# GpSimd takes token differences and two squared keys, and the value stage is put in a new order, in a two-layer kernel on one Trainium2 core

## The chip, the core and the metric

The kernel runs on one core of one Trainium2 chip. The metric is device time in microseconds (us) of one execution. A core has TensorE (PE, matmuls, with PEld for its weight loads), VectorE (DVE), ScalarE (ACT), GpSimd (POOL) and the queues that start transfers (SP). The engines run side by side and wait for each other on semaphores. Each takes its own instructions in the order in which the program lists them, so what stands behind a waiting instruction waits too.

## What is computed

The input is 2048 tokens of 128 channels, kept with channels on the partitions. Four stages follow each other, each with a residual and a layer norm. The change touches the second and its surroundings:

```python
x = _layernorm(x + _L0_attn_ref(x, ...))      # heads attend among themselves; ends in one 128x128 matrix
x = _layernorm(x + _L0_ffn_ref(x, W_r, W_k, W_v, mu_r, mu_k))
x = _layernorm(x + _L1_attn_ref(x, ...))      # two small MLPs, then a scan-like sum over 16 states
x = _layernorm(x + _L1_ffn_ref(x, ...))       # gated MLP with 512 hidden channels, two gelu layers

# _L0_ffn_ref
x_prev = concatenate([zeros, x[:, :-1]])
xr = mu_r * x + (1 - mu_r) * x_prev
xk = mu_k * x + (1 - mu_k) * x_prev
out = sigmoid(xr @ W_r) * (square(relu(xk @ W_k)) @ W_v)
```

## The kernel before, in words

The tokens are cut into four chunks of 512 (`c` = 0 to 3), and every stage works chunk by chunk. There is no planner: the order on each engine is written out by hand as a list of calls, and each call is one or two instructions on one 128x512 tile, with a wait ahead and a semaphore increment behind.

- **First norm (y1).** TensorE makes y1 of a chunk (L212 to L214), ScalarE squares it (`square`, L528), TensorE averages it over the channels (L1235), ScalarE makes 1/sqrt of that by Ln and Exp (`rstd_of`, L533 and L535).
- **Token shift.** For each chunk VectorE does `first_input` (x1 = PSUM times rstd, L887), `token_step` (x1 minus x1 of the token before, L892, both operands in SBUF) and two mixes (L897: step times mu plus x1 of the token before, both tensors in SBUF): the key mix K(c) and the receptance mix R(c). `mixed` counts the mixes.
- **Value stage.** TensorE: `key(c)` (L1255) on K(c), `receptance(c)` (L1259) on R(c), `value(c)` (L1265) on the squared key. ScalarE: `key_relu` (L552), `key_square` (L557), Tanh of the receptance (L547). VectorE: `gate` (L926, L929). Then TensorE centres (`y2`, L1235) and averages the squares (`y2_variance`, L1235), ScalarE does Ln and Exp (L533, L535), VectorE makes x2 and splits it in a high and a low part (`second_input`, L935, L876, L878), on which `layer1(c)` of the third stage starts (L212 to L214).
- **Weights of the last stage.** `wf_raw` holds 11 blocks of 128x512. GpSimd rounds each to its high part (`tensor_copy`, L378 for blocks 0 to 3, L383 for 4 to 10) as soon as the transfer has landed, and VectorE subtracts (`fill_low(f)`, L833, two SBUF operands). ScalarE takes the magnitude of the low parts in four calls (`low_magnitude`, L522). `state_weights` (L851 on VectorE) makes 128x96 matrices for the scan out of a small one. These are put in the gaps of the VectorE and ScalarE lists.
- **Scan.** From about 74 us on GpSimd, VectorE, ScalarE and TensorE share a sum over the states.

Of the kernel before, what the change touches and what calls it, by code (L numbers as in the profile page):

```python
# [23 lines left out]
ALU = mybir.AluOpType  # L24
# [4 lines left out]
CH = 512  # L29
HEADS = 16  # L30
HD = P // HEADS
NS = 16
# [4 lines left out]
LN_EXP = "natural_log_exp_and_others"  # L37
# [7 lines left out]
def build(nc, t, out):  # L45
# [4 lines left out]
    NCH = T // CH  # L50
# [8 lines left out]
    with ctx:  # L59
# [3 lines left out]
        def sem(name):  # L63
            return ctx.enter_context(nc.semaphore(name))
# [39 lines left out]
        nfill = 3 + 2 * KH  # L104
# [13 lines left out]
        def sb_and_f32(name, width):  # L118
# [7 lines left out]
        x1r, x1_f32 = sb_and_f32("x1r", T + 2)  # L126
        xr = sb("xr", [P, 2, T], F32R)
        bx1, bs1, bs2, bs3, bx2, bxt, bdl = [sb(n, [P, T]) for n in ("bx1", "bs1", "bs2", "bs3", "bx2", "bxt", "bdl")]
# [13 lines left out]
                for b in (bx1[:, :], bx2[:, :], bs2[:, :], x1_f32[:, 0, 2:], x1_f32[:, 1, 2:],  # L142
# [31 lines left out]
        sc_mm, sm_ok, smax_ok, exp_ok, srec_ok, prob_ok, u_mm, u_ok, m_mm, mix_ok = [  # L174
            sem(n) for n in ("sc_mm", "sm_ok", "smax_ok", "exp_ok", "srec_ok", "prob_ok", "u_mm", "u_ok", "m_mm",
                             "mix_ok")]
        y1_mm, y1_sq, y1_var, y1_ln, y1_rs, x1_ok, step_ok, mixed = [
            sem(n) for n in ("y1_mm", "y1_sq", "y1_var", "y1_ln", "y1_rs", "x1_ok", "step_ok", "mixed")]
        key_mm, rec_mm, th_ok, relu_ok, k2_ok, v_mm, p_ok, y2_ok, y2_mm, y2_sq, y2_var, y2_ln, y2_rs = [
            sem(n) for n in ("key_mm", "rec_mm", "th_ok", "relu_ok", "k2_ok", "v_mm", "p_ok", "y2_ok", "y2_mm", "y2_sq",  # L180
                             "y2_var", "y2_ln", "y2_rs")]
# [21 lines left out]
        def cs(c):  # L203
            return slice(c * CH, (c + 1) * CH)
# [139 lines left out]
        def _(pool):  # L344
            g = nc.gpsimd
# [31 lines left out]
            for f in range(f0, f1):  # L377
                g.tensor_copy(wf[:, f, 0, :], wf_raw[:, f, :]).then_inc(fill_hi0, 1)  # L378
            pool.wait_ge(fill_hi0, FILL)
            for f in range(FILL, nfill):  # L380
                if f % FILL == 0:
                    pool.wait_ge(ld_f[f // FILL], 16)
                g.tensor_copy(wf[:, f, 0, :], wf_raw[:, f, :]).then_inc(fill_hi, 1)  # L383
            pool.wait_ge(fill_hi, nfill - FILL)

            def c_parts(c):

# [63 lines left out]
            for i in range(NCH // 2):  # L451
                for stage in range(3):
                    for k in range(2):
                        for o in range(KH):
                            n = mtile(i, stage, k, o)
# [9 lines left out]
        def _(act):  # L465
# [50 lines left out]
            def low_magnitude(j):  # L516

                f0, f1 = LOW_SPANS[j]
                act.wait_ge(fill_lo, f1)
                if j:  # L520
                    act.wait_ge(low_ok, j)
                a.activation(magnitudes[:, 0:(f1 - f0) * HID].rearrange("p (f c) -> p f c", c=HID),  # L522
                             full(wf[:, f0:f1, 1, :]), ACT.Abs, accum_out=low_max[:, j:j + 1]).then_inc(low_ok, 1)

            def square(mm_sem, sq_sem, c):

                act.wait_ge(mm_sem, c + 1)
                a.activation(bs1[:, cs(c)], ps[:, 4 + c, :], ACT.Square).then_inc(sq_sem, 1)  # L528
# [14 lines left out]
            def receptance(c):  # L543

                act.wait_ge(rec_mm, c + 1)
                act.wait_ge(y1_var, c + 1)
                a.activation(bs1[:, cs(c)], ps[:, c, :], ACT.Tanh, scale=0.5).then_inc(th_ok, 1)  # L547

            def key_relu(c):

                act.wait_ge(key_mm, c + 1)
                a.activation(bs2[:, cs(c)], ps[:, 4 + c, :], ACT.Relu).then_inc(relu_ok, 1)  # L552

            def key_square(c):

                act.wait_ge(relu_ok, c + 1)
                a.activation(bs3[:, cs(c)], bs2[:, cs(c)], ACT.Square).then_inc(k2_ok, 1)  # L557
# [26 lines left out]
                a.activation(bs1[:, s], bs1[:, s], ACT.Ln, bias=1.0).then_inc(d_ln, count)  # L584

            act.preload_act_table(ACT.Tanh)
            receptance(0)
            key_relu(0)
            key_relu(1)
            key_square(0)  # L590
            receptance(1)
            key_square(1)
            low_magnitude(0)
            receptance(2)
            key_relu(2)
            key_relu(3)
            key_square(2)
            key_square(3)
            receptance(3)
            square(y2_mm, y2_sq, 0)  # L600
            square(y2_mm, y2_sq, 1)
            act.preload_act_table_set(LN_EXP)
            rstd_of(y2_var, y2_ln, y2_rs, 0)
            square(y2_mm, y2_sq, 2)
            rstd_of(y2_var, y2_ln, y2_rs, 1)
# [139 lines left out]
        def _(dve):  # L745
            v = nc.vector
# [80 lines left out]
            def fill_low(f):  # L827

                if f < FILL:
                    dve.wait_ge(fill_hi0, f + 1)  # L830
                else:
                    dve.wait_ge(fill_hi, f - FILL + 1)
                v.tensor_tensor(wf[:, f, 1, :], wf_raw[:, f, :], full(wf[:, f, 0, :]),  # L833
                                ALU.subtract).then_inc(fill_lo, 1)

            dve.wait_ge(sc_mm, 1)
            dve.wait_ge(mask_ok, 2)
            v.scalar_tensor_tensor(sm[:, :], ps[:, 0, 0:P], float(1.0 / np.sqrt(T)), mask[:, :], ALU.mult,
# [8 lines left out]
            def state_weights(n0, n1):  # L847

                dve.wait_ge(h0f_ok, 3)
                for n in range(n0, n1):  # L850
                    v.tensor_scalar(h0sel[:, n, :], h0T[:, :], one_state[:, n:n + 1], None, ALU.mult).then_inc(h0sel_dve, 1)  # L851

            fill_low(0)
            state_weights(9, 11)

            dve.wait_ge(m_mm, 1)
            dve.wait_ge(consts, 6)
# [8 lines left out]
            v.tensor_tensor(w1[:, :, 1, :], w1raw[:, 0:3:2, :], full(w1[:, :, 0, :]), ALU.subtract).then_inc(w1_lo, 1)  # L866
            v.tensor_scalar(amin[:, :], amat[:, :], 0.0, None, ALU.min).then_inc(a_ok, 1)
            v.tensor_scalar(amax[:, :], amat[:, :], 0.0, None, ALU.max).then_inc(a_ok, 1)
            for f in range(1, 5):
                fill_low(f)  # L870

            def split(full_sem, hi_sem, lo_sem, full_buf, dst, c):
# [8 lines left out]
            def shifted(i, c, shift):  # L881
                return x1_f32[:, i, c * CH + shift:(c + 1) * CH + shift]

            def first_input(c):

                dve.wait_ge(y1_rs, c + 1)
                v.tensor_tensor(shifted(0, c, 2), ps[:, 4 + c, :], bs2[:, cs(c)], ALU.mult).then_inc(x1_ok, 1)  # L887

            def token_step(c):

                dve.wait_ge(x1_ok, c + 1)
                v.tensor_tensor(bx2[:, cs(c)], shifted(0, c, 2), shifted(0, c, 1), ALU.subtract).then_inc(step_ok, 1)  # L892

            def token_mix(c, mu, dst):

                dve.wait_ge(step_ok, c + 1)
                v.scalar_tensor_tensor(dst, bx2[:, cs(c)], vec[:, mu:mu + 1], shifted(0, c, 1), ALU.mult,  # L897
                                       ALU.add).then_inc(mixed, 1)

            def mixes(c):  # L900
                token_mix(c, MU_K, bx1[:, cs(c)])
                token_mix(c, MU_R, shifted(1, c, 2))

            first_input(0)
            token_step(0)
            mixes(0)
            first_input(1)
            first_input(2)
            token_step(1)
            mixes(1)  # L910
            first_input(3)
            token_step(2)
            mixes(2)
            token_step(3)
            mixes(3)

            def transformed(c):

# [13 lines left out]
            def second_input(c):  # L932

                dve.wait_ge(y2_rs, c + 1)
                v.tensor_tensor(bx2[:, cs(c)], ps[:, 4 + c, :], bs2[:, cs(c)], ALU.mult).then_inc(x2_ok, 1)  # L935
                split(x2_ok, x2_hi, x2_lo, bx2, lambda c: parts(xr, c), c)

            gate(0)
            gate(1)
            state_weights(11, 12)  # L940
            gate(2)
            gate(3)
            state_weights(12, 14)
            second_input(0)
            second_input(1)
            fill_low(5)
            second_input(2)
            fill_low(6)
            fill_low(7)
            second_input(3)  # L950

            def bounded(c):

# [57 lines left out]

            transformed(0)
            transformed(1)
            fill_low(8)
            bounded(0)
            fill_low(9)
            bounded(1)
            state_weights(14, NS)
            step_size(0)
            c_times_b(0)  # L1020
            step_size(1)
            fill_low(10)
            c_times_b(1)
            dve.wait_ge(a_ok, 2)
            dve.wait_ge(d_ps, 2)
# [158 lines left out]
        def _(pe):  # L1184
# [68 lines left out]
            def key(c):  # L1253
                pe.wait_ge(mixed, 2 * c + 1)
                m.matmul(ps[:, 4 + c, :], w0raw[:, 1, :], bx1[:, cs(c)], start=True, stop=True).then_inc(key_mm, 1)  # L1255

            def receptance(c):
                pe.wait_ge(mixed, 2 * c + 2)
                m.matmul(ps[:, c, :], w0raw[:, 0, :], x1_f32[:, 1, c * CH + 2:(c + 1) * CH + 2], start=True,  # L1259
                         stop=True).then_inc(rec_mm, 1)  # L1260

            def value(c):
                pe.wait_ge(k2_ok, c + 1)
                pe.wait_ge(th_ok, c + 1)
                m.matmul(ps[:, c, :], w0raw[:, 2, :], bs3[:, cs(c)], start=True, stop=True).then_inc(v_mm, 1)  # L1265

            def y2(c):
                over_channels(y2_ok, y2_mm, centre, bs3, 4, c)

            def y2_variance(c):  # L1270
                over_channels(y2_sq, y2_var, ones, bs1, 0, c)
# [92 lines left out]
            key(1)  # L1364
            receptance(1)
            key(2)
            value(0)
            receptance(2)
            value(1)
            key(3)  # L1370
            receptance(3)
            y2(0)
            y2(1)
            value(2)
            value(3)
            y2_variance(0)
            y2_variance(1)
            y2(2)
            y2(3)
            y2_variance(2)  # L1380
            pe.wait_ge(w1_lo, 1)
# [244 lines left out]
```

## Time and profile before

| | us |
|---|---|
| median of the three runs | 255.01 |
| lowest and highest | 253.63 and 256.02 |
| the profiled execution | 255.75 |
| its span, first to last instruction | 254.0 |
| mean granted clock of TensorE, as a share of 2.4 GHz | 0.950 |

The profile has for each engine its busy time and share of the span, the chain of work that ended last (followed back from the last instruction to whatever released it), and a timeline of instructions with their start, duration, and the idle time before them with the engine that ended it. An instruction's duration runs from its start on the engine to its end and takes in any time in which it is held up inside the engine.

### The profile page before, as it was taken

The numbers are of one execution on the slowest core, as the hardware profiler recorded it, in microseconds if no ns is written. First come the engines' busy times: TensorE is split into PE (matmuls) and PEld (weight loads), VectorE is DVE, ScalarE is ACT, GpSimd is POOL, SyncE is SP. The second block draws the span as 40 slices with busy tenths as digits, with TensorE's granted clock in tenths as the row PEclk, the third lists the DMA queues.
The fourth block names the chain that finished last, engine by engine and source line by source line (L and its number), as shares of the span: only waits on it lengthen the run. The fifth ranks groups of instructions, "written<-read, shape, count | busy, mean of one in ns | idle before, by whom it ended". The sixth has DMA issues, their size and how long they took to land.

```text
span 254.0 us, 2617 instructions
## 1 busy us (share of the span) xinstructions
PE 228.5 (90%) x839; PEld 146.9 (58%) x839; DVE 206.9 (81%) x330; ACT 180.5 (71%) x247; POOL 127.1 (50%) x103
## 2 busy tenths in 40 slices
PE   7898888999999659997868999999999899999981
PEld 7898533445542225543434646578888678888860
DVE  3996889596699899969989989980699997996454
ACT  4766499799897999979989956369843743643433
POOL 3362000000079987999999953473344478055220
PEclk9999999999999957999795999999999999999996
DMA  6960000000000000000000000000000000110002
GB/s 135 389 253 1 1 0 0 3 0 0 0 0 0 3 4 0 0 0 0 3 1 1 0 0 0 0 3 0 0 0 3 0 0 0 45 41 0 0 1 83
DMA packets 4847, 6.16 MB, mean 24 GB/s; under 512 B 384, under 2 KB 2656, under 8 KB 4832
## 3 DMA queue, kind: packets, MB, share of 16 engines
q1 hardware_dynamic: 4832, 5.97, 7.1%
q8 instruction: 8, 0.13, 0.2%
q14 instruction: 7, 0.06, 0.1%
HBM read 4.92 MB, written 1.05 MB: 24 GB/s over the span
## 4 chain that ended last, share of the span: by engine, by line
PE 44%; DVE 26%; ACT 9%; POOL 9%; issue 8%; DMA 2%; SPq 0%; ACTq 0%; POOLq 0%; DVEq 0%
PE ps L1454 8%; PE ps L1455 8%; PE ps L1340 7%; PE ps L1316 3%; POOL bs L420 3%; DVE tr L1088 3%; PE ps L1235 2%; DMA bx<-in_x_dram 2%; POOL bxt L399 2%; PE ps L212 2%; DVE xr L1085 2%; DVE tr L1085 2%; PE ps L213 1%; PE ps L214 1%; PE ps L1281 1%
## 5 line engine op out<-in xcount | busy, mean ns | idle before, releaser
L731 ACT ACTIVATE bs<-ps,vec 128x512 f32<-128x512 f32 x48 | 31.7, 691 | 37.2 <-PE ps L1455 36.0
L1316 PE MATMUL ps<-tr,h0sel 96*128 96x512 f32 x64 | 26.5, 527 | 11.0 <-issue 3.0
L389 POOL CAST tr<-bs 96x512 fp32r<-96x512 f32 x4 | 2.8, 695 | 51.1 <-ACT bs L628 50.9
L1316 PEld LDWEIGHTS ps<-tr,h0sel 96*128 96x128 f32 x64 | 12.4, 212 | 24.1 <-issue 12.2
L1454 PE MATMUL ps<-xr,wf 128*128 128x512 f32 x64 | 25.4, 396 | 0.0
L1455 PE MATMUL ps<-xr,wf 128*128 128x512 f32 x64 | 25.3, 396 | 0.0
L460 POOL TENSOR_TENSOR xr<-bs,xr 128x512 fp32r<-128x512 f32 x12 | 16.1, 1349 | 14.0 <-DVE xr L1085 14.0
L460 POOL TENSOR_TENSOR tr<-bs,tr 128x512 fp32r<-128x512 f32 x8 | 10.9, 1360 | 22.3 <-DVE tr L1085 22.3
L1085 DVE CAST tr<-bs 128x512 fp32r<-128x512 f32 x16 | 7.4, 487 | 13.3 <-ACT bs L731 13.2
L460 POOL TENSOR_TENSOR x1r<-bs,x1r 128x512 fp32r<-128x512 f32 x12 | 13.5, 1129 | 9.3 <-DVE x1r L1085 9.3
L445 POOL TENSOR_TENSOR bs<-bs 128x1024 f32<-128x1024 f32 x6 | 14.3, 2384 | 3.7 <-DVE bs L995 3.6
L1454 PE MATMUL ps<-tr,wf 128*128 128x512 f32 x40 | 15.7, 394 | 0.2 <-DVE tr L1088 0.2
L1340 PE MATMUL ps<-bx,centre 128*128 128x512 f32 x28 | 16.0, 706 | 0.0
L1455 PE MATMUL ps<-x1r,wf 128*128 128x512 f32 x40 | 15.7, 393 | 0.0
L1455 PE MATMUL ps<-tr,wf 128*128 128x512 f32 x40 | 15.7, 392 | 0.0
L1454 PE MATMUL ps<-x1r,wf 128*128 128x512 f32 x40 | 15.7, 391 | 0.0
L1454 PE MATMUL ps<-lr,wf 128*128 128x512 f32 x32 | 14.5, 453 | 1.0 <-DVE bs L1070 1.0
L1190 PE MATMUL ps<-ones 128*128 128x128 f32 x86 | 13.0, 314 | 1.1 <-DVE ones L747 1.1
L1455 PEld LDWEIGHTS ps<-xr,wf 128*128 128x128 f32 x64 | 12.0, 188 | 2.9
L1454 PEld LDWEIGHTS ps<-xr,wf 128*128 128x128 f32 x64 | 12.0, 188 | 2.8
L981 DVE SCALAR_TENSOR_TENSOR bx<-ps,amax,bx 128x1024 f32<-128x1024 f32 x11 | 13.6, 1275 | 0.0
L641 ACT ACTIVATE bx<-bdl,amin 128x1024 f32<-128x1024 f32 x12 | 13.0, 1138 | 0.2 <-PE ps L1340 0.2
(221 smaller groups left out, 667.8 us busy)
## 6 DMA issues: line engine op xcount, KB each, us to landing
wf_raw<-in_w_mlp_dram SPq DMA_DIRECT2D x2, 1024.0 KB, 9.2
bx<-in_x_dram SPq DMA_DIRECT2D x4, 256.0 KB, 5.7
out_dram<-bdl SPq DMA_DIRECT2D x4, 256.0 KB, 2.3
wf_raw<-in_w_mlp_dram SPq DMA_DIRECT2D x1, 768.0 KB, 11.8
bdl<-in_w_ssm_dram SPq DMA_DIRECT2D x1, 448.0 KB, 8.5
wa<-in_w_attn_dram SPq DMA_DIRECT2D x1, 256.0 KB, 2.7
w0raw<-in_w_ffn_dram SPq DMA_DIRECT2D x1, 192.0 KB, 7.9
h0T<-in_state_dram SPq DMA_DIRECT2D x1, 48.0 KB, 5.8
```

Source lines behind the costliest of these rows:

```text
L420: g.tensor_tensor(vbuf[e % NB][:, j, :], vbuf[e % NB][:, j, :], zmax, ALU.add).then_inc(e_vp, 1)
L445: g.tensor_tensor(b[:, 0, :], b[:, 0, :], b[:, 1, :], ALU.add).then_inc(e_add, 1)
L460: g.tensor_tensor(sl[:, 1, o, :], hbuf[k][:, o, :], full(sl[:, 0, o, :]), ALU.subtract).then_inc(m_lo_p, 1)
L641: a.activation(vbuf[e % NB][:, j, :], bdl[:, pair_tokens(e)], ACT.Exp, scale=amin[:, n:n + 1]).then_inc(e_t, 1)
L731: a.activation(hbuf[k][:, o, :], ring(mbank(i, stage, k, o)), ACT.Gelu if stage else ACT.Silu, scale=vec[:, s + o:s + o + 1]).then_inc(m_a ...
L981: v.scalar_tensor_tensor(tile, delta_ps, amax[:, n:n + 1], tile, ALU.mult, ALU.add).then_inc(e_v, 1)
L1085: v.tensor_copy(sl[:, 0, o, :], hbuf[k][:, o, :]).then_inc(m_hi, 1)
L1190: last = m.matmul(ps[:, bank, P:2 * P], ones[:, :], ones[:, :], start=True, stop=True)
L1316: last = m.matmul(ps[:, 2 * j + k, :], h0sel[:, group_states(e)[j], :], tr[0:96, 0, cs(2 * (e // NG) + k)], start=True, stop=True)
L1340: last = m.matmul(ps[:, SUM_BANK + k, :], centre[:, :], vbuf[e % NB][:, j, k * CH:(k + 1) * CH], start=(e % NG == 0 and j == 0), stop=(e % ...
L1454: m.matmul(dst, wf[:, f, 0, wo], x[0], start=start, stop=False)
L1455: last = m.matmul(dst, wf[:, f, 0, wo], x[1], start=False, stop=stop and not low_weights)
```

## The change

1. `token_step` of chunks 1 to 3 leaves VectorE. GpSimd makes them (`bx2`), each after `x1_ok` of its chunk, and the mixes of these chunks wait on GpSimd's semaphore `step_pool`. Chunk 0 stays on VectorE.
2. The squared keys of chunks 1 and 3 leave ScalarE. GpSimd multiplies the tile by itself after the relu (`k2_pool`).
3. GpSimd waits for the mixing matrix (`mix_ok` 3) between block 3 and block 4 of its weight copies.
4. VectorE's list has `fill_low` 0 and 1 ahead of the scores, 2 and 3 behind the softmax, 4 to 7 (with five `state_weights`) ahead of `first_input(0)`, and 8 to 10 behind `second_input(3)`; the last one is no longer between the two `c_times_b` ahead of the scan.
5. ScalarE's first `low_magnitude` is ahead of the first norm, and its value stage begins with the keys.
6. VectorE's mixes and TensorE's value stage are in a new order.

```diff
@@ gpsimd
             pool.wait_ge(fill_hi0, FILL)
+            pool.wait_ge(mix_ok, 3)
             for f in range(FILL, nfill):
                 ...
                 g.tensor_copy(wf[:, f, 0, :], wf_raw[:, f, :]).then_inc(fill_hi, 1)
             pool.wait_ge(fill_hi, nfill - FILL)
+            for c in range(1, NCH):
+                pool.wait_ge(x1_ok, c + 1)
+                g.tensor_tensor(bx2[:, cs(c)], x1_f32[:, 0, c * CH + 2:(c + 1) * CH + 2],
+                                x1_f32[:, 0, c * CH + 1:(c + 1) * CH + 1], ALU.subtract).then_inc(step_pool, 1)
+            for c in range(1, NCH, 2):
+                pool.wait_ge(relu_ok, c + 1)
+                g.tensor_tensor(bs3[:, cs(c)], bs2[:, cs(c)], bs2[:, cs(c)], ALU.mult).then_inc(k2_pool, 1)
@@ scalar
+            low_magnitude(0)
             def square(mm_sem, sq_sem, c):
...
             act.preload_act_table(ACT.Tanh)
+            key_relu(0)
+            key_square(0)
+            key_relu(1)
             receptance(0)
-            key_relu(0)
-            key_relu(1)
-            key_square(0)
             receptance(1)
-            key_square(1)
-            low_magnitude(0)
+            key_relu(2)
+            key_square(2)
+            key_relu(3)
             receptance(2)
-            key_relu(2)
-            key_relu(3)
-            key_square(2)
-            key_square(3)
             receptance(3)
             square(y2_mm, y2_sq, 0)
+            act.preload_act_table_set(LN_EXP)
             square(y2_mm, y2_sq, 1)
-            act.preload_act_table_set(LN_EXP)
@@ vector
+            fill_low(0)
+            fill_low(1)
             dve.wait_ge(sc_mm, 1)
...
-            fill_low(0)
-            state_weights(9, 11)
+            fill_low(2)
+            fill_low(3)
...
-            for f in range(1, 5):
+            fill_low(4)
+            state_weights(9, 14)
+            for f in range(5, 8):
                 fill_low(f)
...
             first_input(0)
-            token_step(0)
-            mixes(0)
+            first_step()
+            key_mix(0)
             first_input(1)
+            receptance_mix(0)
             first_input(2)
-            token_step(1)
-            mixes(1)
+            key_mix(1)
+            receptance_mix(1)
             first_input(3)
-            token_step(2)
-            mixes(2)
-            token_step(3)
-            mixes(3)
+            key_mix(2)
+            receptance_mix(2)
+            key_mix(3)
+            receptance_mix(3)
...
             second_input(0)
             second_input(1)
-            fill_low(5)
             second_input(2)
-            fill_low(6)
-            fill_low(7)
             second_input(3)
+            for f in range(8, nfill):
+                fill_low(f)
+            state_weights(14, NS)
...
             step_size(1)
-            fill_low(10)
             c_times_b(1)
@@ tensor
             key(2)
+            receptance(2)
+            key(3)
             value(0)
-            receptance(2)
+            receptance(3)
             value(1)
-            key(3)
-            receptance(3)
+            value(2)
             y2(0)
+            value(3)
             y2(1)
-            value(2)
-            value(3)
             y2_variance(0)
+            y2(2)
             y2_variance(1)
-            y2(2)
             y2(3)
```

## Rows read from the trace of the kernel before

**Rows 1.** The page: busy us of each engine (share of the span) and instructions.

```profile
PE 228.5 (90%) x839; PEld 146.9 (58%) x839; DVE 206.9 (81%) x330; ACT 180.5 (71%) x247; POOL 127.1 (50%) x103
```

**Rows 2.** The chain that ended last, in order of time: start, us, what.

```profile
19.23 0.67 DVE ss L795
19.93 0.59 DVE qkrec L797
...
40.82 1.12 PE ps L1255 x2
...
52.29 0.60 ACT bs L528
...
72.73 1.08 DVE wf L833
...
74.17 0.46 issue
```

**Rows 3.** Timeline, VectorE and GpSimd around 14 and 19 us: start, us, instruction.

```profile
14.24 0.28 DVE L795 TENSOR_SCALAR ss<-ss 128x256 f32<-128x256 f32 x1
14.55 0.29 DVE L797 TENSOR_TENSOR qkrec<-ss 128x128 f32<-128x128 f32 x1
...
18.58 1.79 POOL L383 CAST wf<-wf_raw 128x512 fp32r<-128x512 f32 x3
...
19.23 0.66 DVE L795 TENSOR_SCALAR ss<-ss 128x256 f32<-128x256 f32 x1 [0.48 <-ACT ss L484]
19.93 0.58 DVE L797 TENSOR_TENSOR qkrec<-ss 128x128 f32<-128x128 f32 x1
```

**Rows 4.** Timeline, GpSimd and VectorE, 72 to 74 us.

```profile
71.98 1.28 POOL L391 TENSOR_TENSOR tr<-bs,tr 32x512 fp32r<-32x512 f32 x1
...
72.65 1.17 DVE L833 TENSOR_TENSOR wf<-wf_raw,wf 128x512 fp32r<-128x512 f32 x1
...
73.33 0.96 POOL L389 CAST tr<-bs 96x512 fp32r<-96x512 f32 x1
```

**Rows 5.** Timeline, VectorE and GpSimd in the last stage.

```profile
187.10 0.42 DVE L1085 CAST xr<-bs 128x512 fp32r<-128x512 f32 x1
...
187.26 1.41 POOL L460 TENSOR_TENSOR xr<-bs,xr 128x512 fp32r<-128x512 f32 x1 [2.75 <-DVE xr L1085]
...
187.55 1.67 DVE L1088 TENSOR_TENSOR xr<-bs,xr 128x512 fp32r<-128x512 f32 x1
...
231.17 1.09 POOL L460 TENSOR_TENSOR x1r<-bs,x1r 128x512 fp32r<-128x512 f32 x1 [0.96 <-DVE x1r L1085]
...
236.00 0.69 DVE L1088 TENSOR_TENSOR x1r<-bs,x1r 128x512 fp32r<-128x512 f32 x1
```

**Rows 6.** Timeline, VectorE and ScalarE, 26 to 44 us.

```profile
26.54 0.47 DVE L851 TENSOR_SCALAR h0sel<-h0T,one_state 96x128 fp32r<-96x128 f32 x2
...
28.25 0.42 DVE L866 TENSOR_TENSOR w<-bdl,w 128x256 fp32r<-128x256 f32 x1
...
28.74 2.49 DVE L833 TENSOR_TENSOR wf<-wf_raw,wf 128x512 fp32r<-128x512 f32 x4
32.59 0.69 DVE L887 TENSOR_TENSOR x1r_f<-ps,bs 128x512 f32<-128x512 f32 x1 [1.36 <-ACT bs L535]
34.05 0.75 DVE L897 SCALAR_TENSOR_TENSOR bx<-bx,vec,x1r_f 128x512 f32<-128x512 f32 x1
...
29.39 1.29 ACT L528 ACTIVATE bs<-ps 128x512 f32<-128x512 f32 x2 [2.21 <-PE ps L214]
...
41.61 1.93 ACT L522 ACTIVATE lr_f<-wf 128x2048 f32<-128x2048 f32 x1
```

**Rows 7.** Timeline, ScalarE: the Exp of the second norm, chunk 1.

```profile
53.49 0.63 ACT L535 ACTIVATE bs<-bs 128x512 f32<-128x512 f32 x1
```

**Rows 8.** Windows: stretch, its us, busy time by engine, TensorE's granted clock, DMA share, GB/s.

```profile
122.00:124.00 2.00, 1.86 (x5) 1.48 (x6) 2.00 (x3) 2.00 (x3) 2.00 (x2) 0.68 0.03 8
...
126.00:128.00 2.00, 2.00 (x7) 1.09 (x6) 0.73 (x1) 1.58 (x2) 2.00 (x2) 0.97 0.00 0
```

More of the change, by code:

```diff
@@ L176, in build @@
                              "mix_ok")]
-        y1_mm, y1_sq, y1_var, y1_ln, y1_rs, x1_ok, step_ok, mixed = [
-            sem(n) for n in ("y1_mm", "y1_sq", "y1_var", "y1_ln", "y1_rs", "x1_ok", "step_ok", "mixed")]
+        y1_mm, y1_sq, y1_var, y1_ln, y1_rs, x1_ok, step_ok, mixed, step_pool, k2_pool = [
+            sem(n) for n in ("y1_mm", "y1_sq", "y1_var", "y1_ln", "y1_rs", "x1_ok", "step_ok", "mixed", "step_pool", "k2_pool")]
         key_mm, rec_mm, th_ok, relu_ok, k2_ok, v_mm, p_ok, y2_ok, y2_mm, y2_sq, y2_var, y2_ln, y2_rs = [
@@ L887, in first_input, with first_step, key_mix, receptance_mix @@
                 v.tensor_tensor(shifted(0, c, 2), ps[:, 4 + c, :], bs2[:, cs(c)], ALU.mult).then_inc(x1_ok, 1)
-            def token_step(c):
-                dve.wait_ge(x1_ok, c + 1)
-                v.tensor_tensor(bx2[:, cs(c)], shifted(0, c, 2), shifted(0, c, 1), ALU.subtract).then_inc(step_ok, 1)
+            def first_step():
+                dve.wait_ge(x1_ok, 1)
+                v.tensor_tensor(bx2[:, cs(0)], shifted(0, 0, 2), shifted(0, 0, 1), ALU.subtract).then_inc(step_ok, 1)
             def token_mix(c, mu, dst):
-                dve.wait_ge(step_ok, c + 1)
+                if c:
+                    dve.wait_ge(step_pool, c)
+                else:
+                    dve.wait_ge(step_ok, 1)
                 v.scalar_tensor_tensor(dst, bx2[:, cs(c)], vec[:, mu:mu + 1], shifted(0, c, 1), ALU.mult,
                                        ALU.add).then_inc(mixed, 1)
-            def mixes(c):
+            def key_mix(c):
                 token_mix(c, MU_K, bx1[:, cs(c)])
+            def receptance_mix(c):
                 token_mix(c, MU_R, shifted(1, c, 2))
             first_input(0)
-            token_step(0)
-            mixes(0)
+            first_step()
+            key_mix(0)
             first_input(1)
+            receptance_mix(0)
             first_input(2)
-            token_step(1)
-            mixes(1)
+            key_mix(1)
+            receptance_mix(1)
             first_input(3)
-            token_step(2)
-            mixes(2)
-            token_step(3)
-            mixes(3)
+            key_mix(2)
+            receptance_mix(2)
+            key_mix(3)
+            receptance_mix(3)
             def transformed(c):
@@ L939, in _ @@
             gate(1)
-            state_weights(11, 12)
             gate(2)
             gate(3)
-            state_weights(12, 14)
             second_input(0)
             second_input(1)
-            fill_low(5)
             second_input(2)
-            fill_low(6)
-            fill_low(7)
             second_input(3)
+            for f in range(8, nfill):
+                fill_low(f)
+            state_weights(14, NS)
             def bounded(c):
@@ L1013, in _ @@
             transformed(1)
-            fill_low(8)
             bounded(0)
-            fill_low(9)
             bounded(1)
-            state_weights(14, NS)
             step_size(0)
@@ L1262, in value @@
             def value(c):
-                pe.wait_ge(k2_ok, c + 1)
+                pe.wait_ge(k2_pool if c % 2 else k2_ok, c // 2 + 1)
                 pe.wait_ge(th_ok, c + 1)
```

## Prediction

> **What bounds the kernel now.** I read the page first: TensorE is busy 90% of the span, VectorE 81%, GpSimd 50% [rows 1]. That is an average over stages, so next came the chain in order of time, cut to the stretch that the change touches, 19 to 75 us [rows 2]. It shows four different limits. At 19.2 us the chain is on VectorE, in two small instructions that make the norms of queries and keys. From `first_input(0)` at 32.59 [rows 6] to the key mix of chunk 2 it is VectorE's unbroken list. At 40.82 TensorE takes over with `key(2)` and has no gap until 53.9. Then ScalarE's Ln and Exp of chunk 1 (Exp over at 53.49 + 0.63 = 54.12 [rows 7]) lead to `layer1(1)` on TensorE, which is back to back from there to 75 us. At 72.7 `fill_low(10)` is on the chain, and then the scan begins. All later stages take their start from this one, so I move them rigidly. The price of the change is what it does to that path, in four places. Then I read the timelines of VectorE and GpSimd side by side [rows 3 to 5], since the change puts GpSimd's work beside VectorE's.
>
> **What the trace says of the two engines together.** `fill_low(10)` takes 1.17 us, against 0.68 for the others. It starts at 72.65, GpSimd's subtraction ends at 71.98 + 1.28 = 73.26, and it ends 0.55 behind that, at 73.81. GpSimd's next copy starts at 73.33 and ends 0.47 behind the end of `fill_low(10)` [rows 4]. Likewise the subtraction L1088 takes 1.67 where GpSimd's L460 runs (it ends 0.55 behind L460's end at 188.67), and 0.69 alone; L460 itself waited for VectorE's cast to end at 187.52 and ran 1.15 from there [rows 5]. So one of the two waits for the other's whole instruction. VectorE's operations with an operand in PSUM keep their length under GpSimd work: the rows show blocking where VectorE reads two SBUF tensors (L833, L1088, L797) or scales an SBUF tile by constants (L795: 0.66 against 0.28) [rows 3, 4, 5]. L795 started at 19.23 within a row of GpSimd copies, 0.56 apart, that ended only at 20.37, and was over at 19.89 [rows 3]: it got in between two of them, so they alternate. My prices are, for GpSimd behind VectorE, copy 0.47 and two-operand 1.15 (1.09 - 0.14 = 0.95 where it reads `x1r` [rows 5]); for VectorE behind GpSimd, subtraction 0.55 and mix 0.61 (the mix is 0.75 alone [rows 6], 0.06 above the 0.69 of a subtraction).
>
> **Part 1, the copies move away from 19 us: -0.67.** GpSimd now waits for `mix_ok` behind block 3, so L795 falls from 0.66 to 0.28. L797 has 128 columns against 512 in L1088's 0.69, and 384 columns fewer at (0.69 - 0.28)/384 make it about 0.29 against 0.58 [rows 3, 5]. Both are on the chain [rows 2], 0.38 + 0.29 = 0.67. TensorE has nothing but fillers to do until these are over, so the gain passes.
>
> **Part 2, the copies land beside `fill_low`: +1.66 (bounds +1.2 and +1.66).** `mix_ok` 3 comes while L866 (two SBUF operands) runs, from 28.25 to 28.67 [rows 6]. From there seven copies and `fill_low` 4 to 7 share the access. Copy 4 ends at 28.67 + 0.47 = 29.14, and `fill_low(4)` may not start before it. The two minima of `amat` (scaled by constants, like L795) each let a copy through: copy 5 to 29.65, copy 6 to 30.16, `fill_low(4)` to 30.71. Five `state_weights` at 0.2 (two in 0.47 [rows 6]; per-partition scalars, not blocked) bring VectorE to 31.61; copies 7 (31.18) and 8, freely 0.56 apart [rows 3], end at 31.74. Then `fill_low(5)` 32.29, copy 9 32.76, `fill_low(6)` 33.31, copy 10 33.78, `fill_low(7)` 34.33. `first_input(0)` starts 0.08 ahead of that, at 34.25 instead of 32.59. Before, VectorE had four such subtractions in 2.49 us and then 1.36 idle [rows 6]; that idle time would have covered the work were it not for the copies. If the two minima take no part in the turns, the same count ends at 33.87 and the delay is 1.2; I take the row nearest to them, L795.
>
> `low_magnitude(0)` costs nothing: 1.93 us plus 0.16 to read its sum fits in ScalarE's 2.21 idle ahead of 29.39 [rows 6] once `fill_low(3)` is over just behind the softmax. Without that gap it would cost its 2.1.
>
> **Part 3, steps and squares on GpSimd: +0.91 (bounds +0.7 and +1.5).** I write the list out on the scale of before from 34.25. `first_step` runs from 34.98, K(0) 35.70 to 36.46, `first_input(1)` to 37.06, R(0) to 37.72. GpSimd's step 1 is ready at 37.1, waits for R(0), ends at 37.72 + 0.95 = 38.67. Chunk 2's x1 is there at 38.32, so step 2 follows at once and takes the turn ahead of K(1), which only learns of step 1 then: step 2 ends 39.66, K(1) 39.66 + 0.61 = 40.27, R(1) 40.94, `first_input(3)` 41.54, K(2) 42.21. Step 3 has waited for K(2), ends 43.16, R(2) 43.77. Relu 1 is long done, so GpSimd's square of chunk 1 comes next, 1.15 to 44.92, and K(3) ends at 45.53. Before, K(3) ended at 42.82. TensorE's `key(3)` starts at 45.57 (44.36 before) and nothing behind it waits for VectorE again: eleven products of 0.86 (with 0.1 more for the first; 1.12 with its tail [rows 2]) put `y2_variance(1)` at 54.27 to 55.29, and Ln and Exp end at 56.69 instead of 54.12, +2.57. Of that 1.66 is part 2's, and 0.91 is what the steps and squares cost. The new order of TensorE is in this: it has `y2(2)` one product earlier, and the squares on GpSimd free 1.3 us of ScalarE that nobody waits for. With the square at 0.95 too it is +0.7; with all steps at 1.15 it is +1.5.
>
> What is queued behind: K(1) waits for `step_pool`, and behind it on VectorE stand R(1) and `first_input(3)`, for which step 3 itself waits. That loop, not the 0.6 us a subtraction took on VectorE, sets the pace.
>
> **Part 4, the gaps ahead of the scan: -0.46.** `fill_low(10)` was 1.17 us between the two `c_times_b`. Without it `state_v(0)` starts when TensorE's copy of delta is there, at 74.17; the chain shows the 0.46 from there as issue [rows 2]. Moving blocks 5 to 9 gives nothing: TensorE is back to back from `layer1(1)` to 75 us, and blocks 8 to 10 now lie in VectorE's idle time ahead of `transformed(0)`.
>
> **Sum.** -0.67 + 1.66 + 0.91 - 0.46 = +1.44. The profiled execution took 255.75 (span 254.0 and 1.75 around it), so it would take 257.2; it stood 0.74 above the median of 255.01, so the median would be 256.5. With the bounds of parts 2 and 3, +0.8 to +2.0: 255.8 to 257.1.
>
> The Trainium skill has the rule behind this (SBUF — State Buffer, section "SBUF: two separate sides"): VectorE and GpSimd share a port pair as "an exclusive lock, not a bandwidth split", taken by GpSimd's instructions and by VectorE's with two SBUF inputs or in a two-port mode. The rows on L1088 and L833 agree. It also counts the mixes (two SBUF tensors and a scalar), of which no row of before shows one beside GpSimd. By the rule the sum is +1.44, and were the mixes exempt it would be the second rival's.
>
> **Rivals.**
> - *The clock falls.* TensorE would stand idle from rec(0)'s end at 38.9 until K(1) at 40.3, after shorter gaps. In the scan the granted clock fell to half after longer pauses of TensorE; one such fall shows 0.68 at 122 to 124 us and 0.97 again at 126 to 128 [rows 8], 3.4 us at half. Here it would cost between nothing (while TensorE waits anyway) and 1.7 us: about 258.0.
> - *The mixes don't take turns with GpSimd.* Then steps run beside them, 1.28 each. With VectorE starting on time, K(2) is over at 39.45 and `key(2)` starts at 39.49 instead of 40.82 (-1.33); `y2(2)` stands one product (0.86) earlier on TensorE, of which ScalarE's own list lets 0.44 through, so Exp 1 ends 1.77 earlier. With part 2's delay: -0.67 + 1.66 - 1.77 - 0.46 = -1.24, so 253.8. Against it: their operands are those of L1088, two SBUF tensors.
> - *The other side: the change does what it is written for.* VectorE's instructions in a row keep the port and GpSimd's copies wait, so part 2 costs nothing, and the steps too slip in free: -0.67 - 1.77 - 0.46 = -2.9, so 252.1. It decides from the point where `first_input(0)` still starts when its rstd is there. Against it speaks L795, let in between two copies, and L460, let in behind a cast.
>
> **How the numbers follow.** Chances: my forecast 0.55, the clock's fall 0.18, mixes exempt 0.14, all free 0.13. The time predicted is the likeliest case's, 256.5. The range leaves out most of the last case and the far end of the clock's: 253.2 to 258.4. Over or under 1% is about what a measurement of this kernel tells from no change, so the bounds are 252.5 and 257.6. Slower takes two thirds of the clock case and a tenth of the forecast's: 0.18, faster most of the last case: 0.12, and within 1% the rest, 0.70.
>
> **What would show it.** L795 and L797 at 0.28 and 0.29. `fill_low` 5 to 7 each at 1 us or so beside copies of 0.6 to 1.0, no idle time ahead of `first_input(0)`. Mixes of chunk 1 to 3 above 0.75 and up to 2 us, each ending 0.6 behind a GpSimd instruction. `key(3)` at about 44.9 on the new scale (45.57 - 0.67), `layer1(1)` at 58.0. `c_times_b(1)` 0.7 behind `step_size(1)`. Mixes of 0.75 throughout, or idle time ahead of `first_input(0)`, would prove me wrong.

## The result, and the profile after

| | before | after |
|---|---|---|
| median of 20 runs, us | 254.89 | 256.57 |
| lowest and highest | 253.33 and 256.18 | 255.33 and 258.41 |
| ratio of after to before, 95% interval | | 1.0067 [1.0047, 1.0088] |
| profiled execution, span | 255.75, 254.0 | 256.97, 255.2 |

The change makes the kernel 1.7 us slower. The predicted median was 256.5, with +1.44 as the sum. I read the trace of after between two marks that hold everything the change touches: the start of the first small norm instruction (19.23 before [rows 3], 18.91 after) and the start of the first `state_v` (74.63 before, where the issue time in [rows 2] ends, 75.33 after). The stretch grew from 55.40 to 56.42, +1.02.

Timeline of VectorE in the changed kernel (start, us, instruction; lines are those of the new file: L804 and L806 are the norm instructions, L842 the low parts, L862 `state_weights`, L900 `first_input`, L905 the step, L913 the mixes, L998 `state_v`):

```profile
18.91 0.29 DVE L804 TENSOR_SCALAR ss<-ss 128x256 f32<-128x256 f32 x1 [0.48 <-ACT ss L494]
19.24 0.29 DVE L806 TENSOR_TENSOR qkrec<-ss 128x128 f32<-128x128 f32 x1
...
27.07 0.29 DVE L874 TENSOR_TENSOR mixr<-mix,mixr 128x128 fp32r<-128x128 f32 x1
27.28 0.42 DVE L877 TENSOR_TENSOR w<-bdl,w 128x256 fp32r<-128x256 f32 x1
27.61 0.59 DVE L878 TENSOR_SCALAR amin<-vec 128x16 f32<-128x16 f32 x1
...
28.21 1.08 DVE L842 TENSOR_TENSOR wf<-wf_raw,wf 128x512 fp32r<-128x512 f32 x1
29.21 2.14 DVE L862 TENSOR_SCALAR h0sel<-h0T,one_state 96x128 fp32r<-96x128 f32 x5
31.28 1.88 DVE L842 TENSOR_TENSOR wf<-wf_raw,wf 128x512 fp32r<-128x512 f32 x3
33.08 0.68 DVE L900 TENSOR_TENSOR x1r_f<-ps,bs 128x512 f32<-128x512 f32 x1
33.79 0.94 DVE L905 TENSOR_TENSOR bx<-x1r_f 128x512 f32<-128x512 f32 x1
...
37.72 1.51 DVE L913 SCALAR_TENSOR_TENSOR bx<-bx,vec,x1r_f 128x512 f32<-128x512 f32 x1 [0.33 <-POOL bx L389]
39.15 0.74 DVE L913 SCALAR_TENSOR_TENSOR x1r_f<-bx,vec,x1r_f 128x512 f32<-128x512 f32 x1
39.81 0.68 DVE L900 TENSOR_TENSOR x1r_f<-ps,bs 128x512 f32<-128x512 f32 x1
40.41 0.74 DVE L913 SCALAR_TENSOR_TENSOR bx<-bx,vec,x1r_f 128x512 f32<-128x512 f32 x1
41.07 1.52 DVE L913 SCALAR_TENSOR_TENSOR x1r_f<-bx,vec,x1r_f 128x512 f32<-128x512 f32 x1
42.52 1.52 DVE L913 SCALAR_TENSOR_TENSOR bx<-bx,vec,x1r_f 128x512 f32<-128x512 f32 x1
...
75.33 1.28 DVE L998 SCALAR_TENSOR_TENSOR bx<-ps,amax,bx 128x1024 f32<-128x1024 f32 x1 [0.69 <-PE ps L1372]
```

GpSimd in the same kernel (L384 the copies of blocks 4 to 10, L389 the steps, L394 the squares):

```profile
30.84 2.80 POOL L384 CAST wf<-wf_raw 128x512 fp32r<-128x512 f32 x1
...
36.27 2.41 POOL L389 TENSOR_TENSOR bx<-x1r_f 128x512 f32<-128x512 f32 x2 [2.08 <-DVE x1r_f L900]
40.57 1.48 POOL L389 TENSOR_TENSOR bx<-x1r_f 128x512 f32<-128x512 f32 x1 [1.89 <-DVE x1r_f L900]
42.01 1.48 POOL L394 TENSOR_TENSOR bs<-bs 128x512 f32<-128x512 f32 x1
45.94 1.04 POOL L394 TENSOR_TENSOR bs<-bs 128x512 f32<-128x512 f32 x1 [2.44 <-ACT bs L564]
```

The reader is to see three things. The norm instructions are short (0.66 and 0.58 in [rows 3]). The 1.36 us that VectorE had idle ahead of `first_input(0)` [rows 6] are gone: it starts 6.01 behind L874, against 4.55 before. And three mixes last 1.5 instead of 0.75, each ending 0.55 behind an instruction of GpSimd: K(1) at 39.23 behind 38.68, R(2) at 42.60 behind 42.05, K(3) at 44.04 behind 43.49. GpSimd waits in turn: its third step starts at 40.57, K(2) is over at 41.15, and it ends 0.90 later.

The chain (start, us, what) now changes over to GpSimd and back where before it was VectorE alone:

```profile
35.52 0.61 DVE x1r_f L900
...
36.27 1.42 POOL bx L389
...
37.72 1.51 DVE bx L913
39.23 0.66 DVE x1r_f L913
39.89 0.60 DVE x1r_f L900
40.49 0.66 DVE bx L913
41.15 0.97 DVE x1r_f L913
42.12 0.40 issue
42.52 1.53 DVE bx L913
...
44.10 1.12 PE ps L1268 x2
```

### The profile page after: what moved, and what is told of

The parts are those of the page before. It is cut to its first block, busy times and chain, and to the rows that moved or that the text cites. A ratio compares the mean times of both kernels' runs of the same rounds, so it can differ in the third digit from the quotient of the medians.

```text
span 255.2 us, 2617 instructions
## 1 busy us (share of the span) xinstructions
PE 228.2 (89%) x839; PEld 145.6 (57%) x839; DVE 208.4 (82%) x327; ACT 180.4 (71%) x245; POOL 136.4 (53%) x108
## 4 chain that ended last, share of the span: by engine, by line
PE 46%; DVE 27%; POOL 9%; issue 8%; ACT 6%; DMA 1%; ACTq 0%; POOLq 0%; DVEq 0%
PE ps L1467 8%; PE ps L1468 8%; PE ps L1353 7%; PE ps L1329 3%; POOL bs L430 3%; PE ps L1248 3%; DVE tr L1101 2%; DVE bx L913 2%; PE ps L212 2%; POOL bxt L409 2%; DVE xr L1098 2%; DVE tr L1098 2%; POOL tr_f L422 1%; PE ps L214 1%; PE ps L213 1%
## 5 line engine op out<-in xcount | busy, mean ns | idle before, releaser
L998 DVE SCALAR_TENSOR_TENSOR bx<-ps,amax,bx 128x1024 f32<-128x1024 f32 x11 | 13.6, 1278 | 0.7 <-PE ps L1372 0.7
L384 POOL CAST wf<-wf_raw 128x512 fp32r<-128x512 f32 x7 | 6.7, 1003 | 14.0 <-DVE mixr L874 14.0
```

The lines of the kernel that those rows point to most:

```text
L998: v.scalar_tensor_tensor(tile, delta_ps, amax[:, n:n + 1], tile, ALU.mult, ALU.add).then_inc(e_v, 1)
```

## The experiments

My theory was that of the prediction: VectorE's instructions on SBUF and GpSimd's take turns, whole instructions at a time. Rivals were that GpSimd is merely slow and VectorE waits for its results, and that the new orders are themselves the loss. A single run scatters by 3 us, but in the trace the stretch between the two marks repeats within 0.02 (53.91 twice for one kernel, 56.42 and 56.41 for another), so I judge by it and give the ratio beside it. Where copies run at 19 us it is less sure: whether a copy catches the first norm instruction or not is worth 0.37 (0.66 or 0.29, see idle_steps). Column three is the time from L874's counterpart to `first_input(0)`, column four from there to the end of K(3), column five the last output transfer from issue to landing.

| kernel | between the marks | to first_input(0) | to K(3)'s end | last transfer | ratio, 95% interval |
|---|---|---|---|---|---|
| before | 55.40 | 4.55 | 10.23 | 2.3 | 1 |
| the change | 56.42 | 6.01 | 10.96 | 2.8 | 1.0067 [1.0047, 1.0088] |
| changed_again | 56.41 | 6.01 | 10.95 | 2.7 | 1.0066 [1.0034, 1.0099] |
| no_hold | 55.41 | 4.55 | 10.72 | 2.7 | 1.0010 [0.9969, 1.0051] |
| steps_back | 56.39 | 6.01 | 10.92 | 2.8 | 1.0023 [0.9984, 1.0061] |
| squares_back | 55.81 | 6.01 | 10.17 | 2.3 | 1.0032 [0.9989, 1.0074] |
| orders_only | 54.54 | 4.55 | 9.90 | 2.3 | 0.9964 [0.9921, 1.0006] |
| short_hold | 53.91 | 4.56 | 9.91 | 2.3 | 0.9963 [0.9932, 0.9994] |
| short_hold_again | 53.91 | 4.55 | 9.90 | 2.3 | 0.9948 [0.9920, 0.9975] |
| idle_steps | 56.60 | 4.55 | 12.32 | 2.3 | 1.0077 [1.0036, 1.0117] |
| write_only | 54.60 | 4.55 | 9.90 | 2.3 | one execution |
| hold_only | 55.50 | 5.19 | 10.39 | 2.3 | 1.0008 [0.9975, 1.0042] |
| weights_last | 57.05 | 6.88 | 10.71 | 2.7 | one execution |
| weights_first | 56.24 | 5.59 | 11.19 | 2.9 | one execution |

**no_hold** takes the hold of the copies out of the changed kernel.

```diff
             pool.wait_ge(fill_hi0, FILL)
-            pool.wait_ge(mix_ok, 3)
```

> The changed kernel, but GpSimd copies blocks 4 to 10 as soon as they have landed (at 16 to 20 us, as before) instead of behind the mixing matrix. Theory of turns (GpSimd and two-operand VectorE work wait for each other): the two small norm instructions at 19 us go back to 0.66 and 0.58 (+0.65), first_input(0) starts again when its rstd is there (-1.46) and first_step is 0.69 instead of 0.94 (-0.25), so 1.06 us less than the changed kernel: about 255.5, ratio to before near 1.002. Rival (GpSimd is simply a slow engine for the steps, and its copies disturb nobody): no difference from the changed kernel, 256.6.

Measured: 1.01 less than the change between the marks (1.06 expected), median 255.46 against 255.39 for before. The norm instructions are blocked again:

```profile
19.23 0.69 DVE L803 TENSOR_SCALAR ss<-ss 128x256 f32<-128x256 f32 x1 [0.48 <-ACT ss L493]
19.95 0.57 DVE L805 TENSOR_TENSOR qkrec<-ss 128x128 f32<-128x128 f32 x1
...
32.61 0.69 DVE L899 TENSOR_TENSOR x1r_f<-ps,bs 128x512 f32<-128x512 f32 x1 [0.39 <-ACT bs L546]
```

So the hold gives 0.66 at 19 us and loses 1.7 at 28 us. `first_input(0)` is again released by ScalarE, after 0.39 idle: without copies beside it the new list of low parts fits.

**steps_back, squares_back and orders_only** undo the GpSimd work in parts; in the last both are undone and the hold too.

```diff
# steps_back
-            for c in range(1, NCH):            # gpsimd
-                pool.wait_ge(x1_ok, c + 1)
-                g.tensor_tensor(bx2[:, cs(c)], ..., ALU.subtract).then_inc(step_pool, 1)
             receptance_mix(0)                  # vector; the same for 2 and 3
+            token_step(1)
             first_input(2)
# squares_back
-            for c in range(1, NCH, 2):         # gpsimd
-                pool.wait_ge(relu_ok, c + 1)
-                g.tensor_tensor(bs3[:, cs(c)], bs2[:, cs(c)], bs2[:, cs(c)], ALU.mult).then_inc(k2_pool, 1)
             key_relu(1)                        # scalar; the same for 3
             receptance(0)
+            key_square(1)
```

> The changed kernel with the three token differences back on VectorE; squares of chunks 1 and 3 and the hold of the copies stay. Theory of turns: three subtractions of 0.60 come back on VectorE, the three turns of about 0.95 behind GpSimd go, but the square of chunk 1 still blocks one mix for about 1.15: the key mix of chunk 3 ends 11.3 us behind the start of first_input(0), against 10.96 in the changed kernel, so about +0.3: 256.9. Rival (what costs is that the mixes wait for a slow GpSimd step, the squares are free): it ends 10.2 us behind, 0.7 less: 255.9.

> The changed kernel with the squared keys of chunks 1 and 3 back on ScalarE; the steps stay on GpSimd and the hold stays. Theory of turns: the key mix of chunk 3, which was 1.53 us behind the square, falls to 0.75, so 0.77 less: 255.8. Rival (the squares on GpSimd are hidden, since TensorE needs them late): no difference, 256.6, or more if ScalarE becomes late.

> The new orders of all engines and the new places of the low parts, but steps on VectorE, squares on ScalarE and the copies not held: only the orders of the change are left. Theory of turns: the key mix of chunk 3 ends 9.9 us behind the start of first_input(0) (10.23 before), the Exp of the second norm's chunk 1 ends 21.05 behind it (21.53 before), and the gap ahead of the scan gives 0.38: 0.86 less than before, 254.0, ratio 0.9966. Rival (the new orders are themselves the loss): above before, 255.5 or more.

Measured: with the steps back nothing changes (56.39; K(3) ends 10.92 behind, not the 10.2 of the rival, nor quite the 11.3 I expected). Three subtractions on VectorE cost what three turns on GpSimd cost. With the squares back K(3) takes 0.74 as an ordinary mix and ends 0.79 earlier. The stretch is only 0.61 shorter (0.77 was expected), because TensorE becomes the limit: K(3) is over at 43.52, but `key(3)` starts at 43.87, straight behind `receptance(2)`. The rival "hidden squares" expected 0. The orders alone are 0.86 shorter than before, to the hundredth what was expected, so the new orders are a gain; the third theory falls. Steps and squares together cost 0.87 (55.41 minus 54.54). Most of that is the square of chunk 1: with the steps alone on GpSimd K(3) ends 10.17 behind, which is the 9.90 of the orders alone plus the 0.25 by which the last held copy lengthens the first step. Moving the steps gained VectorE nothing, and what they cost in the whole is the small rest, 0.26. The ratios of these three runs have intervals that hold 1 and don't tell the kernels apart; the trace does.

**idle_steps and write_only** measure the disputed cost by itself. To the kernel with the orders only, GpSimd gets three instructions whose results nobody reads: subtractions in the one, memsets of the same tile in the other.

```diff
+            for c in range(1, NCH):
+                pool.wait_ge(x1_ok, c + 1)
+                g.tensor_tensor(bxt[:, cs(c)], x1_f32[:, 0, ...], x1_f32[:, 0, ...],
+                                ALU.subtract).then_inc(step_pool, 1)      # idle_steps
+                g.memset(bxt[:, cs(c)], 0.0).then_inc(step_pool, 1)       # write_only
```

> The kernel with the orders only, plus three subtractions on GpSimd whose results nobody reads, each started by the x1 of chunks 1 to 3; VectorE still makes the steps itself, and waits for GpSimd only 20 us later. Nothing on the path depends on GpSimd. Theory of turns: each subtraction blocks one VectorE instruction for about 0.87, so the key mix of chunk 3 ends 12.5 us behind the start of first_input(0) instead of 9.9, and the whole is 2.6 us longer than with the orders only: about 256.7. Rival (GpSimd's steps cost only because VectorE's mixes wait for their results): 9.9 and 254.1.

> The kernel with idle subtractions on GpSimd, but each subtraction replaced by a memset of the same 128x512 tile: GpSimd writes and reads nothing. If a GpSimd instruction takes turns only where it reads SBUF, the key mix of chunk 3 ends 9.9 us behind the start of first_input(0), as with the orders only, and no mix is above 0.75. If any GpSimd instruction takes turns, each memset holds one VectorE instruction for most of its own length, and the mix ends between 10.5 and 12 behind.

Measured: the idle subtractions make the stretch 2.06 longer than the orders alone, and K(3) ends 12.32 behind instead of 9.90 (12.5 expected). Expected between the marks was 2.6: in this execution the short norm instruction escaped the copies (0.29), which is 0.37 of the difference. With memsets nothing moves. VectorE and GpSimd of idle_steps, then of write_only, at the same place in the list (K(1), then R(1)):

```profile
37.55 0.74 DVE L908 SCALAR_TENSOR_TENSOR bx<-bx,vec,x1r_f 128x512 f32<-128x512 f32 x1
38.21 1.52 DVE L908 SCALAR_TENSOR_TENSOR x1r_f<-bx,vec,x1r_f 128x512 f32<-128x512 f32 x1
...
37.70 1.48 POOL L388 TENSOR_TENSOR bxt<-x1r_f 128x512 f32<-128x512 f32 x1 [1.23 <-DVE x1r_f L898]
```

```profile
37.32 0.74 DVE L907 SCALAR_TENSOR_TENSOR bx<-bx,vec,x1r_f 128x512 f32<-128x512 f32 x1
37.98 0.75 DVE L907 SCALAR_TENSOR_TENSOR x1r_f<-bx,vec,x1r_f 128x512 f32<-128x512 f32 x1
...
37.47 0.53 POOL L388 MEMSET bxt<- 128x512 f32 x1 [1.27 <-DVE x1r_f L897]
```

Both times GpSimd starts about 0.15 us after VectorE has begun a mix. The subtraction ends 0.90 behind the mix, and VectorE's next mix, which has nothing to do with it, takes 1.52 and ends 0.55 behind the subtraction. The memset takes its 0.53 inside the mix, as all three do, and the next mix takes 0.75. So the cost is one of access, not of data. The memset, which reads nothing, does not wait for VectorE; the copies, which read and are hardly longer (0.61), do. The other direction was hardly tried: the memsets were over, but for 0.07 us at most, when VectorE's next instruction started. The Trainium skill (SBUF — State Buffer, section "SBUF: two separate sides") says the same: VectorE's instructions with two SBUF inputs are shut out "only against a GpSimd op that reads SBUF". The 0.53 of the memset and the 1.52 of the mix agree with it.

**hold_only, weights_last and weights_first** ask how the turns are taken. The first is the kernel before with the hold alone. The others are the changed kernel with the five `state_weights` behind `fill_low` 4 to 7, or ahead of 4.

```diff
# weights_last
-            fill_low(4)
+            for f in range(4, 8):
+                fill_low(f)
             state_weights(9, 14)
-            for f in range(5, 8):
-                fill_low(f)
# weights_first
-            fill_low(4)
             state_weights(9, 14)
-            for f in range(5, 8):
+            for f in range(4, 8):
                 fill_low(f)
```

> The kernel before with the one added wait: GpSimd's copies of blocks 4 to 10 wait for the mixing matrix. All orders, steps and squares as before. Strict alternation: the two norm instructions give 0.65 back, seven copies alternate with fill_low 1 to 4, first_input(0) starts 5.7 behind the mixing matrix's low part instead of 4.55 (+1.1), sum +0.5: 255.9 against 255.4. If VectorE keeps its turn for instructions in a row, it starts at 4.6 to 5.0 and the sum is about -0.4.

> The changed kernel, with the five state_weights behind fill_low 4 to 7 instead of between 4 and 5. In the changed kernel GpSimd's copy of block 9 waited 2.3 us while five VectorE instructions in a row went first, against strict alternation. If turns alternate here (one copy, one low part, about 1.02 a pair), first_input(0) starts about 7.0 us behind the low part of the mixing matrix (6.0 in the changed kernel). If VectorE keeps its turn as soon as it has instructions in a row, it starts about 5.0 behind. Time: about 1 us above or below the changed kernel.

> The changed kernel with the five state_weights ahead of fill_low 4. Strict alternation: five state_weights each behind a copy, then four low parts, first_input(0) starts about 6.3 us behind the low part of the mixing matrix (6.0 in the changed kernel, 6.9 with the weights last). If a run of state_weights is what lets VectorE keep its turn (as it did from the third on in the changed kernel), the last two and all four low parts go at their free length and one copy waits almost 3 us: about 5.6.

Measured, VectorE in hold_only, then VectorE and GpSimd in weights_first:

```profile
28.67 4.15 DVE L834 TENSOR_TENSOR wf<-wf_raw,wf 128x512 fp32r<-128x512 f32 x4
32.74 0.68 DVE L888 TENSOR_TENSOR x1r_f<-ps,bs 128x512 f32<-128x512 f32 x1
```

```profile
28.75 2.15 DVE L862 TENSOR_SCALAR h0sel<-h0T,one_state 96x128 fp32r<-96x128 f32 x5
30.82 2.48 DVE L842 TENSOR_TENSOR wf<-wf_raw,wf 128x512 fp32r<-128x512 f32 x4
...
30.38 3.40 POOL L384 CAST wf<-wf_raw 128x512 fp32r<-128x512 f32 x1
```

Low parts and copies alternate strictly: four low parts take 4.15 in hold_only where they took 2.49 in [rows 6], 1.02 a pair. `first_input(0)` is 0.64 later than before; the norms give 0.66 back, the last copy lengthens the first step (K(3) ends 0.16 later), and the stretch is 0.10 longer, where I expected 0.5. I had counted seven copies ahead of `first_input(0)` and expected +1.1; only six stand there. `state_weights` behave otherwise. The first three wait for a copy each (0.64 against 0.28), and from the third on VectorE keeps its turn through everything in its list, while one copy waits 3.40 us (2.80 in the changed kernel, where the three waited too). 5.59 was expected as 5.6 for that case and 6.3 for alternation. With the weights last it is 6.88, as alternation has it; there two `state_weights` waited and then the copies had run out. What lets VectorE keep the turn from the third on is open: in the changed kernel the fourth of them started 0.05 behind the start of a copy, exactly as the second and third had, which were held.

**short_hold** puts what I had learnt together: the orders only, and the copies of blocks 8 to 10 held just past the norm instructions.

```diff
             for f in range(FILL, nfill):
+                if f == 2 * FILL:
+                    pool.wait_ge(nrm_step, 5)
                 if f % FILL == 0:
                     pool.wait_ge(ld_f[f // FILL], 16)
```

> The kernel with the orders only (steps on VectorE, squares on ScalarE, copies early), plus one thing: GpSimd's copies of blocks 8 to 10 wait until the two small norm instructions at 19 us are over, and run beside VectorE's reciprocal and PSUM work. Theory of turns: the two small instructions fall to 0.29 each (-0.66) and nothing else moves, so 1.5 us below before: 253.5 or a ratio of 0.994. Rival (the hold of the copies costs wherever it is put): no gain over the orders alone, 254.1.

> The same kernel as short_hold (orders only, copies of blocks 8 to 10 held past the two norm instructions), timed once more for a narrower interval: 1.5 us below before by the trace, ratio 0.994. Rival: within its interval of no change.

Measured: 53.91 between the marks, 1.49 less than before, and the two timings give 0.9963 and 0.9948, both with their intervals wholly below 1: about 1.2 us faster than before and, by the ratios, some 3 us faster than the change. The 0.63 that the short hold gives over the orders alone is read from the trace; the ratios (0.9964 for the orders) can't tell it from nothing. GpSimd's copies, in two rows with the norm instructions between:

```profile
16.60 2.29 POOL L385 CAST wf<-wf_raw 128x512 fp32r<-128x512 f32 x4 [2.02 <-DMA wf_raw<-in_w_mlp_dram]
20.15 1.74 POOL L385 CAST wf<-wf_raw 128x512 fp32r<-128x512 f32 x3 [1.25 <-DVE qkrec L801]
...
19.46 0.29 DVE L799 TENSOR_SCALAR ss<-ss 128x256 f32<-128x256 f32 x1 [0.48 <-ACT ss L487]
19.79 0.29 DVE L801 TENSOR_TENSOR qkrec<-ss 128x128 f32<-128x128 f32 x1
```

**changed_again** asks for the part of the loss that the marks don't hold.

> The changed kernel as it is, once more. From the first small norm instruction at 19 us to the first state_v its trace was 1.02 us longer than before, and behind that nothing moved by more than 0.1, while the medians stood 1.68 apart. If the path between the two marks is all there is, the ratio is near 1.004 and the stretch is again 56.4 against 55.4; if the change costs something outside it, the ratio is again near 1.007, and the trace should show another stretch that is longer.

Measured: 1.0066 again, 1.7 us, with +1.01 between the marks. The other stretch is the very end. Transfers at the end, first in the changed kernel (251.2 to 255.2 us), then in the kernel before (250.8 to 254.0 us):

```profile
q1 hardware_dynamic: 1056, 0.52, 41.7%
q14 instruction: 1, 0.01, 1.1%
...
out_dram<-bdl SPq DMA_DIRECT2D x1, 256.0 KB, 2.8
```

```profile
q1 hardware_dynamic: 1014, 0.50, 49.2%
...
out_dram<-bdl SPq DMA_DIRECT2D x1, 256.0 KB, 2.3
```

A fetch of instructions falls into the last output transfer, which lands 0.5 later. In the 14 traces it is there in the six with the squares on GpSimd, and the transfer takes 2.7 to 2.9; it is absent in the other eight, 2.3 in each. My first reading, the length of GpSimd's program, does not fit: squares_back (106 instructions of GpSimd in its profile) and idle_steps (106) are without the fetch, steps_back (105) has it. What goes with it in all 14 is ScalarE's count, 245 instructions with the squares on GpSimd and 247 without. In the kernel before the last fetch of the same queue comes at 241.7 us, 9.6 ahead of the last output transfer; in the changed kernel it comes at 252.9, 0.9 after that transfer was issued. So it seems to be one fetch that comes later when ScalarE's list is two instructions shorter, but no run changes that alone. So the trace holds +1.02 and +0.48, 1.50, within the interval of the ratio (1.2 to 2.2 us).

## Why the prediction was right, point by point

- **Part 1, -0.67:** measured -0.65 (0.29 and 0.29 against 0.66 and 0.58). Right.
- **Part 2, +1.66:** `first_input(0)` came 1.46 later, and the last copy held `first_step` for another 0.25 (0.94 against 0.69), +1.71. The sum is right by errors that cancel, which is luck. I had the minimum and the maximum of `amat` each let a copy through: only the first of the two was held (0.59, the other 0.16), so `fill_low(4)` was over 0.44 sooner than I had it. I took `state_weights` as not blocked: three of the five were, and the five took 2.06 instead of 0.98. I took strict alternation for `fill_low` 5 to 7: they ran at 0.60 each, 1.80 where I had 2.64, counted from the end of the weights. The 0.25 on `first_step` was not in the sum at all.
- **Part 3, +0.91:** from the start of `first_input(0)` to the end of the Exp of chunk 1 it was 21.53 before [rows 6, 7] and 22.12 after; without the 0.25 of part 2 that is +0.34, below the lower bound of +0.7. The orders alone give 0.46 of gain in this stretch (21.07), so steps and squares cost 0.80. The mechanism was right, instruction by instruction: step 2 ahead of K(1), R(2) behind step 3, K(3) behind the square. The size was too large. A square on GpSimd takes 1.04 undisturbed and 0.90 behind a wait, where I had 1.15; each of the two steps that waited 0.90 against 0.95; a mix behind GpSimd 0.55, not 0.61, three times. That is 0.25, 0.10 and 0.18 of the 0.57. My prices came from the pairs [rows 4, 5] at other places of the kernel.
- **Part 4, -0.46:** from the Exp to `state_v`, 20.51 before and 20.12 after, -0.39; TensorE's copy of delta became the last to arrive.
- **What is missing from the sum:** the instruction fetch at the end, +0.48, which no step of mine had. It fills what part 3 was too large by. The median fits the prediction to 0.1, and 0.12 of that comes from the base, 255.01 in three runs against 254.89 in twenty: the change itself was predicted as +1.44 and measured as 1.7 by the ratio, 1.50 by the trace. The steps, taken one by one, don't fit. The path and the turns were right; that the total came so close is luck.
- **The clock** did not fall. In the window where I had feared it, TensorE was busy for 4.61 of 6 us at the full granted clock:

```profile
36.00:42.00 6.00, 4.61 (x10) 1.27 (x8) 5.67 (x8) 4.43 (x7) 3.84 (x3) 1.00 0.00 0
```

- **Mixes exempt** fell by the three mixes of 1.5. **All free** fell by `first_input(0)`: it started without idle time ahead. Its mechanism, VectorE keeping the turn, exists all the same, from the third of the `state_weights` on.

## What to carry to other kernels

Before moving elementwise work to GpSimd, look at what VectorE does at that moment: an instruction of VectorE on two SBUF tensors, or one that works on an SBUF tensor and a constant or per-partition scalar, as the first norm instruction and `state_weights` do, and a GpSimd instruction that reads SBUF run one after the other. Each idle subtraction, which ran 0.90 us behind its wait, cost VectorE 0.80 (2.42 for three). A subtraction moved over was then no gain, since VectorE lost what it had saved, and a square moved over from ScalarE was a loss. GpSimd's reading work belongs beside VectorE's work on PSUM, its reciprocals and its idle time (in short_hold the reciprocal of 0.95 and the products of 0.69 kept their length beside copies); holding it back by one well-placed wait gave 0.63 us here, and a wait that held it too long gave 0.66 and took 1.7. A list of several edits can hide gains as well: the orders were worth 0.86 and stood under a loss of 1.9.

## What was not expected of the hardware

- A GpSimd memset of 128x512 runs its 0.52 us inside a two-operand instruction of VectorE, where a copy or a subtraction waits for that instruction's end; VectorE's instructions beside it keep 0.69 and 0.74.
- `state_weights` (one SBUF tensor scaled by a per-partition scalar, one each 0.2 us when unblocked) also wait for GpSimd's copies, 0.64 each, and after the third VectorE keeps its turn for up to six more instructions while a copy waits 3.4 us. This came in both arrangements that had at least three of them beside the copies.
- Single executions differ by whether TensorE's granted clock falls around 124 us in the scan. It did in the two profiles compared here, in changed_again, orders_only and weights_last, where 179.3 to 179.9 us lie between `state_v` and the end, and not in the other nine, with 177.4 to 178.6. The windows of the changed kernel and of no_hold:

```profile
124.00:126.00 2.00, 2.00 (x4) 0.88 (x3) 2.00 (x3) 2.00 (x2) 2.00 (x2) 0.50 0.00 0
```

```profile
124.00:126.00 2.00, 2.00 (x7) 0.96 (x6) 2.00 (x3) 2.00 (x2) 1.92 (x3) 1.00 0.00 0
```

From `state_v` to the end the changed kernel took 179.9 and no_hold 177.7, with the same program there. That is larger than the whole effect of the change, and the reason why the marks were needed.
